# Moving one row-block turn and one row statistics to later slots of a fused decoder kernel

## The reference

```python
# decoder layer, per sequence; 16 heads of width 32
ln_out = layernorm(x);  q, k, v = split(ln_out @ w_qkv + b_qkv)
x = x + attention(q, k, v, ltor_mask) @ w_ao + b_ao
ln_out = layernorm(x);  q = ln_out @ w_q + b_q;  k, v = split(ctx @ w_kv + b_kv)
x = x + attention(q, k, v, cross_mask) @ w_co + b_co
x = x + gelu(layernorm(x) @ w1 + b1) @ w2 + b2
# non-local block over channels
W = (theta @ x)^T (phi @ ctx) / 512;  y = W (g @ ctx)^T
out = batchnorm(w @ y) + x
```

## Time and profile before

| | us |
|---|---|
| time, median of 3 runs (2007.12 to 2007.95) | 2007.74 |
| time of the profiled execution | 2011.13 |
| its span by the profile | 2009.3 |
| PE busy | 1976.2 (98%) |
| DVE busy | 1470.8 (73%) |
| ACT busy | 1162.6 (58%) |
| POOL busy | 550.2 (27%) |
| granted TensorE clock | 0.999 of full speed |

### The profile page before, as it was taken

The page is one execution under the profiler, slowest core; times in us unless marked ns, Lnnn a source line. Parts: engine busy times, 40 slices in busy tenths (PEclk is TensorE's granted clock), DMA queues, the critical chain, the costliest instruction groups (busy, mean ns, idle before and its releaser), DMA issues. The chain is left out here.

```text
span 2009.3 us, 41550 instructions
## 1 busy us (share of the span) xinstructions
PE 1976.2 (98%) x13632; PEld 1570.0 (78%) x13632; DVE 1470.8 (73%) x3868; ACT 1162.6 (58%) x3251; POOL 550.2 (27%) x556
## 2 busy tenths in 40 slices
PE   9999999999999999999999998999999999999998
PEld 8877777777776777777777776888888888888887
DVE  7799999999999999899899888564444343435333
ACT  4388878888888888888888788421111121212111
POOL 1012222222224344323423432053132131313000
PEclk9999999999999999999999999999999999999999
DMA  8546667567668867767767734531212212121201
GB/s 279 168 94 139 146 165 155 128 168 161 135 173 193 195 172 173 168 162 180 176 152 183 170 90 116 171 107 35 79 42 68 68 47 78 47 63 52 61 24 48
DMA packets 681720, 252.67 MB, mean 126 GB/s; under 512 B 533312, under 2 KB 626112, under 8 KB 681536
## 3 DMA queue, kind: packets, MB, share of 16 engines
q1 hardware_dynamic: 535616, 195.84, 38.5%
q10 hardware_dynamic: 145920, 54.55, 11.2%
HBM read 167.41 MB, written 82.84 MB: 125 GB/s over the span
## 5 line engine op out<-in xcount | busy, mean ns | idle before, releaser
L1309 ACT ACTIVATE A_p<-A_p,A_nmax 128x256 f32<-128x256 f32 x1024 | 507.1, 500 | 5.4 <-DVE A_res L1634 1.7
L1666 DVE CUSTOM_DVE_ANT_0 A_p<-A_p,A_ma 128x256 f32<-128x256 f32 x1024 | 376.6, 423 | 4.6
L1656 DVE TENSOR_TENSOR A_p<-A_sc,A_mk 128x1024 f32<-128x1024 f32 x256 | 312.3, 1220 | 48.0 <-PE A_tp L1071 47.4
L820 POOL TENSOR_TENSOR A_ct_l<-A_cx,A_ct_h 128x256 fp32r<-128x256 f32 x122 | 114.3, 937 | 652.3 <-DVE A_nmax L1666 639.1
L1368 ACT ACTIVATE A_pt<-A_tp 128x512 f32<-128x512 f32 x396 | 218.5, 588 | 47.2 <-PE A_tp L1071 45.9
L1071 PEld LDWEIGHTS A_tp<-A_ident,A_p 128*128 128x128 f32 x1584 | 178.8, 141 | 71.2 <-ACT A_p L1309 33.0
L1071 PE MATMUL A_tp<-A_ident,A_p 128*128 128x128 f32 x1584 | 222.5, 277 | 1.5 <-DVE A_xt_l L1617 0.7
L1505 ACT ACTIVATE A_mk<-A_tp,A_cols 128x512 f32<-128x512 f32 x62 | 42.8, 690 | 269.1 <-PE A_tp L68 269.0
L1309 ACT ACTIVATION_READ_ACCUMULATOR A_p<-A_p,A_nmax 128x1 f32 x1024 | 197.2, 193 | 0.0
L1505 ACT ACTIVATE A_ma<-A_tp,A_cols 128x512 f32<-128x512 f32 x62 | 42.8, 690 | 242.5 <-PE A_tp L68 242.5
L66 PE MATMUL A_banks<-A_xt_h,A_w_h 128*128 128x512 f32 x384 | 162.2, 422 | 3.4 <-DVE A_res L1634 2.1
(11 more groups left out here) (248 smaller groups left out, 5001.7 us busy)
## 6 DMA issues: line engine op xcount, KB each, us to landing
exponentials<-A_ln_shift SPq DMA_DIRECT2D x464, 64.0 KB, 2.7
A_pt<-exponentials SPq DMA_DIRECT2D x116, 256.0 KB, 3.1
A_rt<-inverses SPq DMA_DIRECT2D x512, 32.0 KB, 2.4
x<-A_res SPq DMA_DIRECT2D x64, 256.0 KB, 3.6
A_res<-x ACTq DMA_DIRECT2D x58, 256.0 KB, 4.1
turned<-A_x ACTq DMA_DIRECT2D x224, 64.0 KB, 2.8
A_x<-x SPq DMA_DIRECT2D x54, 256.0 KB, 3.7
A_x<-x ACTq DMA_DIRECT2D x42, 256.0 KB, 3.1
```

Source lines behind the costliest of these rows:

```text
L820: pool.tensor_tensor(ct_l[:, f, part], cx[:, :], f32(ct_h[:, f, part]), ALU.subtract).then_inc(c_lo, 1)
L1309: act.activation(p[:, g % 2, j, t, :], p[:, g % 2, j, t, :], ACT.Exp, scale=-1.0, bias=nmax[:, g % 2, j, t:t + 1], accum_out=rsum[:, g % 2 ...
L1656: dve.tensor_tensor(p[:, g % 2, heads, :, :].rearrange("p j t s -> p j (t s)"), sc[:, heads, :], m, ALU.mult)\
L1666: dve.tensor_tensor_reduce(out=a_, in0=a_, in1=ma[:, b, t, :], scale=-1.0, scalar=BIG, op0=ALU.add, op1=ALU.min, accum_out=nmax[:, g % 2, ...
```

## The change

The four turns of a body's row tiles on DVE stood two in slot 3 and two in slot 4. They now stand one in slot 3, two in slot 4 and one, at the very end, in slot 5. The writes on ACT stood two tiles in slot 4 and two in slot 5. They are now one in slot 4, two in slot 5 and one in slot 6 (behind its first four exponentials). The statistics of row tile 0 stood in slot 0; in bodies 2 to 15 they are now made at the end of slot 6 of the body before. The SP queue's order and all waits of other engines are as they were.

```diff
@@ exponential (ACT) @@
-                if by_blocks(k) and h in (4, 5):
-                    write_block(k, r, 2 * h - 8 + n // 4, n % 4)
+                tile = {(4, 0): 0, (5, 0): 1, (5, 1): 2, (6, 0): 3}.get((h, n // 4))
+                if by_blocks(k) and tile is not None:
+                    write_block(k, r, tile, n % 4)
@@ (DVE) @@
+            def row_blocks(r, t):
+
+                dve.wait_ge(ln_x, (r + 1) * TT + (t + 1))
+                dve.transpose(x[:, t, :], x[:, t, :]).then_inc(a_blk, 1)
+
@@ slot (DVE) @@
-                if by_blocks(k) and h in (3, 4) or k == NU - 1 and 3 <= h < 3 + TT:
-                    for t in (2 * h - 6, 2 * h - 5) if by_blocks(k) else (h - 3,):
-                        dve.wait_ge(ln_x, (r + 1) * TT + (t + 1))
-                        dve.transpose(x[:, t, :], x[:, t, :]).then_inc(a_blk, 1)
+                if k == NU - 1 and 3 <= h < 3 + TT:
+                    row_blocks(r, h - 3)
+                if by_blocks(k):
+                    for t in {3: (0,), 4: (1, 2)}.get(h, ()):
+                        row_blocks(r, t)
                 if k < NU and h in ((0, 1) if k else (1, 2)):
-                    row_statistics(r + 1, 0 if h == (0 if k else 1) else 2)
+                    if h != 0 or k < 2:
+                        row_statistics(r + 1, 0 if h == (0 if k else 1) else 2)
                     row_statistics(r + 1, 1 if h == (0 if k else 1) else 3)
...
                 for n in chunk_at.get((k, h), ()):
                     split_chunk(n)
+                if by_blocks(k) and h == 5:
+                    row_blocks(r, 3)
+                if by_blocks(k) and h == 6:
+                    row_statistics(r + 2, 0)
```

## The result

| | before | after |
|---|---|---|
| median, us (6 runs each, side by side) | 2007.85 (2006.35 to 2009.31) | 2015.01 (2012.31 to 2018.02) |
| ratio, 95% interval | | 1.0037 [1.0024, 1.0050] |
| profiled execution, us | 2011.13 | 2013.83 |
| its span, us | 2009.3 | 2012.0 |

The change makes the kernel slower: 7 us (0.37%), with 4.8 to 10 in the interval. The forecast was 2012.7 us in a range up to 2018.0. So I read both kernels from more than one profile: three of before (the one shown, and two more, r1 and r3, 2006.97 and 2009.51 us) and two of after (r2, 2014.13 us).

A forecast was written before the change was run, and what follows sets the result against it. PE, busy 98% of the span, was taken as the bound, with a floor of 8.90 us per slot. The terms -6.4 - 0.8 + 12.2 = +5.0 us gave a median of 2012.7 us, range 2011.7 to 2018.

The forecast's parts named there:

- The gain of slot 3: One DVE turn leaves slot 3, so PE waits less for the low part of k: 6.4 us won, bounds 0 and 8.35.
- Rival (c): Slot 3 gains nothing because ACT's high part of k or the spread inverses end the same pause: 2019.1 us, chance 0.04.
- The gain of slot 0: Row tile 0's statistics, 0.68 us of DVE work, leave slot 0: 0.8 us won, bounds 0 and 0.9.
- The costs put at nothing: DVE's idle time covers the turn ending slot 5 (0.62 us) and the statistics ending slot 6 (0.68 us): cost 0.
- ACT's new wait: Tile 3's first write waits for the turn ending slot 5; copies of probabilities may start 0.3 us late: cost 0.
- The loss in slots 6 and 7: Four writes entering slot 6 delay SP's urgent exponentials load and inverses store: 12.2 us lost, bounds 0 and 21.0.
- D: Delay of SP's queue in slot 6 caused by the four writes, taken as 1.0 us.
- 11 D + 3 (D - 0.6): Loss in slots 6 and 7: 11 bodies without slack pay D, bodies 4, 5 and 6 only what exceeds 0.6 us.
- rival (a): Partial contention in slot 6, D between 0.3 and 0.9 us, so gain and loss cancel: 2007.1 us, chance 0.33.
- free room is 4% of the slot: Slot 6's DMA engines have 0.37 us free of 9.25, leaving 1.26 of the writes' 1.63 us as delay.
- The sign in PE's product with v: In slot 6 it should show waits for the exponentials of 0.3 us and more in most bodies.
- rival (d): All four writes go ahead of both urgent transfers in slot 6: D = 1.63, loss 21.0, 2021.5 us; chance 0.06.

The follow-up runs named there:

- e1: Kernel before with only row tile 0's statistics moved from slot 0 to the end of slot 6 of the body before; 2008.06 us, ratio 0.9992.
- e5: Kernel after, but from body 2 on tile 3's writes move a sixteenth of their bytes, waits and issues kept; 2004.18 us, ratio 0.9973 to before.
- e3: Kernel before with only the writes moved: one tile in slot 4, two in slot 5, one in slot 6; 2018.01 us, ratio 1.0043.
- e8: Kernel after with tile 3's writes behind the second four exponentials of slot 6 instead of the first four; 2022.38 us, ratio 1.0058 to before.
- e4: Kernel before with tiles 2 and 3 both written in slot 6, one tile each in slots 4 and 5; 2044.98 us, ratio 1.0175.
- e6: Kernel before with one of slot 3's two turns issued behind the low part of k instead of ahead, no DMA moved; 2004.77 us, ratio 0.9975.

## Why the prediction was right, step by step

**The gain of slot 3** was put at 6.4 us and measured at 6.1; after's slots 3 sum to 125.6 where 126.5 was named, and PE's waits for k fell as said. Rival (c) is out: nothing else ended that pause.

**The gain of slot 0** was put at 0.8 us. The means give 0.8, but e1 shows that it can't be told from nothing.

**The costs put at nothing.** DVE's idle time before slots 6 and 7 of body 12 is 0.60 and 0.63 us, as worked out. ACT's new wait, 26.5 us in all, costs nothing that e5 shows; PE waited for it in one body, in place of another wait. It was the largest new row in the view of waits and had hardly a part in the loss.

**The loss in slots 6 and 7** was put at 12.2 us and measured at 11.0. The mechanism is shown from three sides: the move of the writes alone brings the loss (e3), without their bytes it goes (e5), and behind the two urgent transfers they leave slot 6 alone (e8). The prediction put a price on four writes in slot 6. e4 says that the price depends on what slot 5 has queued: with four there instead of eight, the store is no later than in before.

**The size is in part luck.** D, the lateness of the store of the inverses, was put at 1.0 us. It was 0.5 us in the mean of all bodies (7.0 to 7.5), and 0.6 without body 7, whose slots 4 and 6 are long in every profile. The store in body 10 landed 6.3 us after its issue, where 6.0 was named, but it went from 5.3 to 5.8 in the mean. By my formula, 11 D + 3 (D - 0.6), a D of 0.6 makes a loss of 6.6 us and no net difference: that is rival (a), to which I gave 0.33. The time came out as forecast because the other factor missed the other way. I had each microsecond of D cost one in 11 bodies and hardly anything in three. Measured, the 11 bodies lost 8.6 us (0.78 each, not 1.0), and the three lost 2.4 (0.8 each, not 0.4). So 0.6 us of D cost 0.79 us in each body.

Two things go with that, and neither is proved to be the reason. The last of the loads of the spread inverses, behind the store, landed 0.7 us later in the mean (10.7 to 11.4 after the start of slot 6), since they too share the engines with the writes. And bodies 4, 5 and 6 had little reserve: in the profile of before their slots 6 and 7 took 17.80 us each, the floor; in after 18.19, 18.20 and 18.88, in r2 18.57, 19.15 and 18.87. That a slot sits at the floor says that it isn't late, not by how much it could be later. The loss isn't even either: between the means of the profiles it runs from 0.07 us in body 1 to 1.5 in bodies 2 and 8, so that no single lateness accounts for each body.

The step "free room is 4% of the slot" failed too. In body 12 of after the two queues' shares are 73.2% and 34.0%, more than the whole, so packets overlap in time and the shares don't add up to a capacity. I take that for a reason why D came out below 1.26; no run tests it. The sign in PE's product with v also came only in part: 7 waits, 3.3 us, where most bodies were named and before already had 2 waits, 2.1 us. The inverses, not the exponentials, were the chain that mattered.

The Trainium skill, page "DMA: Bandwidth & Descriptors", section "Queues, rings and completion order", has the engines take turns between queues packet by packet. What is seen goes with it in kind: neither queue waited out the other, and both were slowed in body 12, SP's store by 0.6 us and the writes from 2.1 us in slot 4 to 5.1. It does not go with it in the size that I drew from it for rival (d): 1.63 us of writes made the urgent chain 0.5 to 0.7 us late, under half of that, and in e4, with eight writes in the two slots instead of twelve, the store was 0.3 us earlier than in before.

**Left open.** The forecast was 5.0 us more than before. The timed difference is 7 us (4.8 to 10), the slots of the bodies account for 3.9 and the profiled executions for 4.8. Profiles of the same kernel differ by up to 5 us (1015.7 and 1020.5 us for the bodies of before), so the rest may be sampling, but I can't show it. Nor is it settled why the statistics add nothing to e6. That the writes of slot 5 count as well is read from e4 against e3 alone, and a kernel that makes use of it, with four writes in slot 5, four in the first half of slot 6 and none behind them, wasn't run. Nor was one in which SP's store stands ahead of slot 5's backlog.

## What to carry to other kernels

When a step moves to a slot in which its engine is idle, the transfers that hang on it move too: look at the DMA engines, at what the slot before has already queued on them, and at the small urgent transfers of the slot of arrival before counting the gain. If the step is only in the way of one instruction, issue it right behind that instruction; this won 5.3 of the 6.4 us here and moved no transfer (e6). And don't take the largest new wait for the cause: keep the wait and remove the bytes, and see which of them the time follows.

## What the hardware showed

Four writes of 64 KB in 128-byte pieces, behind eight others and beside a full queue, made a 16 KB store on another queue land 0.5 us later in the mean (0.6 in body 12), and needed 5.1 us themselves instead of 2.1. With four others ahead instead of eight the store landed 6.7 us after the start of its slot, against 7.0 with eight others and none of the four. Four writes behind the store made the four 32 KB loads that follow it take 3.3 us instead of 2.2 (e8). And the two queues' shares of the engines can sum to 107%.
